# Layer 0's cross attention: scores from queries taken through the key weights, against the context itself

## The reference

```python
xn = _layernorm(x, ln_gamma, ln_beta)
q = (xn @ w_q).reshape(B, SQ, NUM_HEADS, DIM_HEAD)
kv = context @ w_kv
k, v = jnp.split(kv, 2, axis=-1)
scores = jnp.einsum('bqhd,bkhd->bhqk', q * SCALE, k)
attn = jax.nn.softmax(scores, axis=-1)
out = jnp.einsum('bhqk,bhkd->bqhd', attn, v).reshape(B, SQ, INNER)
out = out @ w_out + b_out
return out * jnp.tanh(gate[0])
```

## Time and profile before

| | us |
|---|---|
| median of 3 runs | 1728.44 (1726.32 to 1729.37) |
| the profiled execution | 1730.11 |
| its span, first to last instruction | 1728.2 |
| start of the first matmul | 9.08 |
| first scores of the attention loop | 65.55 |
| scores of the 31st unit | 488.65 |

### The profile page before, as it was taken

The page is one execution under the profiler, slowest core; times in us unless marked ns, Lnnn a source line. Parts: engine busy times, 40 slices in busy tenths (PEclk is TensorE's granted clock), DMA queues, the critical chain, the costliest instruction groups (busy, mean ns, idle before and its releaser), DMA issues.

```text
span 1728.2 us, 27121 instructions
## 1 busy us (share of the span) xinstructions
PE 1679.0 (97%) x10603; PEld 1290.0 (75%) x10603; DVE 980.5 (57%) x1999; ACT 791.9 (46%) x1564; POOL 234.0 (14%) x317
## 2 busy tenths in 40 slices
PE   7999999999999999998999999999999899999997
PEld 5577777777757766564999986677767678799996
DVE  4243344434346686522766665565554776598885
ACT  3333333333324345520655564454445443477774
POOL 0100000000001301313111102211100304021111
PEclk9999999999999999999999999999999999999999
DMA  6020110102042003033999973111231052599994
GB/s 252 1 98 30 45 45 30 49 26 75 24 159 98 1 1 120 28 124 134 343 389 389 392 273 104 32 62 34 84 123 49 25 213 101 206 354 363 362 363 105
DMA packets 43805, 246.52 MB, mean 143 GB/s; under 512 B 5801, under 2 KB 6305, under 8 KB 20624
## 3 DMA queue, kind: packets, MB, share of 16 engines
q1 hardware_dynamic: 31392, 216.63, 33.3%
q0 software_dynamic: 7664, 19.68, 4.1%
q10 hardware_dynamic: 4608, 8.33, 1.3%
HBM read 229.01 MB, written 16.13 MB: 142 GB/s over the span
## 4 chain that ended last, share of the span: by engine, by line
PE 92%; DVE 3%; DMA 2%; ACT 1%; issue 1%; POOL 1%; SPq 0%; POOLq 0%; DVEq 0%; ACTq 0%
PE bank L648 29%; PE bank L268 12%; PE bank L2380 7%; PE bank L274 5%; PE bank L791 3%; PE bank L3453 3%; PE bank L819 3%; PE bank L745 2%; PE bank L2931 2%; PE bank L1490 2%; PE bank L738 2%; PE bank L1174 2%; PE bank L1989 2%; PE bank L1991 2%; PE bank L1990 2%; PE bank L1547 1%
## 5 line engine op out<-in xcount | busy, mean ns | idle before, releaser
L648 PE MATMUL bank<-split 128*128 128x512 f32 x2196 | 530.4, 396 | 1.3 <-ACT arena L674 1.3
L648 PEld LDWEIGHTS bank<-split 128*128 128x128 f32 x2196 | 404.3, 188 | 99.3 <-issue 9.5
L268 PE MATMUL bank<-arena,weights 128*128 128x128 f32 (+1 forms) x1032 | 136.1, 290 | 10.8 <-DMA weights<-in_L_xattn_w_kv 9.1
L268 PEld LDWEIGHTS bank<-arena,weights 128*128 128x128 f32 x1032 | 123.8, 193 | 24.3 <-issue 12.9
L799 ACT COPY normed<-bank 128x512 f32<-128x512 f32 x128 | 68.9, 592 | 150.4 <-PE bank L791 150.4
L762 DVE TENSOR_REDUCE small<-bank 128x1 f32<-128x512 f32 x64 | 43.9, 686 | 151.8 <-PE bank L738 151.8
L680 DVE COPY arena<-bank 128x512 f32<-128x512 f32 x76 | 52.5, 691 | 120.8 <-PE bank L648 120.8
L674 ACT COPY arena<-bank 128x512 f32<-128x512 f32 x76 | 44.5, 586 | 152.8 <-PE bank L648 114.3
L2380 PE MATMUL bank<-up_high_r,tok_r 128*128 128x352 f32 x512 | 108.2, 323 | 0.0
L274 PE MATMUL bank<-weights,arena 128*128 128x512 f32 x224 | 101.7, 604 | 0.9 <-issue 0.9
L781 ACT ACTIVATE normed<-bank,small 128x512 f32<-128x512 f32 x64 | 44.1, 689 | 124.0 <-DVE small L764 123.7
(11 more groups left out here) (404 smaller groups left out, 3092.6 us busy)
## 6 DMA issues: line engine op xcount, KB each, us to landing
weights<-in_L_ffn_re_w SPq DMA_DIRECT2D x62, 1024.0 KB, 10.6
weights<-in_L_w SPq DMA_DIRECT2D x20, 1408.0 KB, 13.1
arena<-in_ctxT SPq DMA_DIRECT2D x24, 1024.0 KB, 5.0
arena<-in_L_w SPq DMA_DIRECT2D x12, 1408.0 KB
weights<-in_L_w_full SPq DMA_DIRECT2D x10, 1280.0 KB, 10.6
weights<-in_L_ffn_sw SPq DMA_DIRECT2D x9, 1024.0 KB, 4.7
expert_out<-arena ACTq DMA_DIRECT2D x31, 256.0 KB, 8.3
arena<-in_L_w_full SPq DMA_DIRECT2D x6, 1280.0 KB
```

The lines of the kernel that those rows point to most:

```text
L268: s = pe.matmul(out, w[:, k, j0:j0 + m], rhs(k), start=(k == 0), stop=(k == KT - 1))
L648: s = pe.matmul(bank[:, :], still, moving, start=(n == 0), stop=(n == len(order) - 1))
```

## The change

Instead of projecting the context to keys, the kernel multiplies the queries by the transposed key weights of each head. What comes out, `through_keys` (for each sequence and head 512 x 64, split into halves), is the stationary side of the scores, and the split context itself is the moving side. The scores are thus the same sums in another order.

- The host lays the key half of `w_kv` out transposed and by rows (`L0_xattn_w_kT`), the value half as before (`L0_xattn_w_v`).
- Key groups g = 0 to 3 are gone in layer 0; each unit projects two value groups.
- `through_keys_tensor(c, z)` is new: 16 fp32 matmuls with 64 rows x 128 columns of key weights stationary and a head's 64 queries moving. Even heads are on rows 0 to 63, odd heads on rows 64 to 127, into two banks. Two such calls make a step's operand; ACT and DVE split each bank into high and low halves (entries "qw" of the split order). In the loop each call is made for the step after the present one.
- `scores_tensor` makes two groups of 12 matmuls 128 x 512, one for each of banks 3 and 4, each with its own count in `scored`. A head pair now lies in one bank, where before each bank held every second head.
- On DVE the values copy and the "qw" low halves stand ahead of the value groups' copies; the context of the next step but one is split in one go in each step's second unit.
- The start: context 0 and the first value weights come in eight slices of 256 KB with a semaphore each; value groups of step 0 are computed slice by slice into banks 0 to 3 (`first_values_tensor`). x, query and key weights are asked for right behind. All four value groups stand ahead of the transposes, and queries with two through_keys calls between them behind.
- The second half of the key weights is loaded behind context 9, once the calls of steps 0 to 7 are done.

```diff
+            for k in range(2):
+                for m in range(KT):
+                    for s in range(2):
+                        r, o = s * half, (k * KT + m) * SEQ
+                        last = pe.matmul(halves[s][:, o:o + SEQ], w.view[r:r + half, m, (2 * z + k) * P:(2 * z + k + 1) * P],
+                                         self.qT[r:r + half, self.tile_of(c, m), b * SEQ:(b + 1) * SEQ], start=True, stop=True)
+            last.then_inc(self.qw_mm.sem, 1)
...
+                order = [(k, a, b) for k in range(KT) for a, b in ((0, 0), (0, 1), (1, 0))]
+                for i in range(2):
+                    m = 2 * u + i
+                    if n >= 1:
+                        pe.wait_ge(self.exped.sem, self.exped.at(2 * n - 1 + i))
+                    for j, (k, a, b) in enumerate(order):
+                        last = pe.matmul(banks[3 + i][:, :], self.through_keys[c % 2][a][:, k, m * P:(m + 1) * P],
+                                         self.split_ctx[c % 2][b][:, k, :], start=(j == 0), stop=(j == len(order) - 1))
+                    last.then_inc(self.scored.sem, 1)
...
-                        last = pe.matmul(banks[3 + s][i * half:(i + 1) * half, :],
-                                         self.qT[r:r + half, self.tile_of(c, 2 * u + i), b * SEQ:(b + 1) * SEQ],
-                                         self.kT[c % len(self.kT)][r:r + half, 2 * u + i, :], start=True, stop=True)
...
+                if self.layer == 0 and c + 1 < self.steps:
+                    self.through_keys_tensor(pe, c + 1, u)
...
+                    if c == NSEQ + 1:
+                        sp.wait_ge(self.qw_mm.sem, self.qw_mm.at(2 * NSEQ))
+                        load_weight(sp, "x0_k1")
...
-        x0.load_context(sp, 0)
-        load_weight(sp, "x0_k0")
-        load_weight(sp, "x0_v0")
-        sp.wait_ge(x0.kv_mm.sem, x0.kv_mm.at(1))
-        sp.wait_ge(x0.low.sem, x0.low.at(x0.ctx_split(0)))
-        x0.load_context(sp, 1)
+        values = weights["x0_v0"]
+        for k in range(KT):
+            c = slice(k * DIM, (k + 1) * DIM)
+            sp.dma_start(x0.ctxT[:, k, :], A["ctxT"][0][:, k, :]).then_inc(slice_in[k], 16)
+            sp.dma_start(wslot[values.slot][:, c], values.source[:, c]).then_inc(slice_in[KT + k], 16)
         for i in range(NT):
             sp.dma_start(x[:, i, :], A["x"][:, i, :]).then_inc(x_in[i], 16)
         load_weight(sp, "x0_q0")
+        load_weight(sp, "x0_k0")
         load_weight(sp, "x0_q1")
+        sp.wait_ge(x0.low.sem, x0.low.at(x0.ctx_split(0)))
+        x0.load_context(sp, 1)
...
+        x0.first_values_tensor(pe)
         pe.wait_ge(consts, IDENT)
...
-        for g in (2 * KT - 2, 2 * KT - 1):
-            x0.kv_tensor(pe, 0, g)
         pe.wait_ge(first_xnT, KT)
-        x0.queries_tensor(pe, range(x0.tiles))
+        x0.queries_tensor(pe, range(5))
+        x0.through_keys_tensor(pe, 0, 0)
+        x0.queries_tensor(pe, (5,))
+        x0.through_keys_tensor(pe, 0, 1)
+        x0.queries_tensor(pe, (6, 7))
```

More of the change, by code:

```diff
@@ L540, in __init__ @@
                 if layer == 0:
-                    count = KT
-                    splits = [("ctx", c + 2, 2 * u), ("ctx", c + 2, 2 * u + 1)]
+                    count = KT // 2
+                    splits = [("qw", c + 1, u, s) for s in range(2)] + [("ctx", c + 2, k) for k in range(KT) if u == 1]
                 else:
@@ L651, in kv_bank, with first_values_tensor, through_keys_tensor @@
         def kv_bank(self, c, g):
+            if self.layer == 0 and c == 0:
+                return banks[g - KT]
             return banks[self.place["kv", c, g] % 3]
+        def first_values_tensor(self, pe):
+            for k in range(KT):
+                pe.wait_ge(self.low.sem, self.low.at(self.split_no["w", "v", 0, k]))
+                for g in range(KT, 2 * KT):
+                    for a, b in ((0, 0), (0, 1), (1, 0)):
+                        s = pe.matmul(self.kv_bank(0, g)[:, :], self.split_ctx[0][a][:, k, (g - KT) * P:(g - KT + 1) * P],
+                                      self.split_v[b][:, k, :], start=(k == 0 and a == b == 0), stop=(k == KT - 1 and a == 1))
+                    if k == KT - 1:
+                        s.then_inc(self.kv_mm.sem, 1)
+        def through_keys_tensor(self, pe, c, z):
+            w = weights[f"x0_k{c // NSEQ}"]
+            if c % NSEQ == 0:
+                pe.wait_ge(w.landed, w.value)
+                pe.wait_ge(self.q_a.sem, self.q_a.at(self.tile_of(c, KT)))
+            halves = [self.bank_free(pe, self.place["qw", c, z, s]) for s in range(2)]
+            b, half = c % NSEQ, P // 2
+            for k in range(2):
[5 more added lines that the diff above has]
+            last.then_inc(self.qw_mm.sem, 1)
         def kv_out(self, e, c, g, bank):
-            e.wait_ge(self.kv_mm.sem, self.kv_mm.at(2 * KT * c + g + 1))
+            e.wait_ge(self.kv_mm.sem, self.kv_mm.at(self.per_step * (c + 1) - 2 * KT + g + 1))
             if g < KT:
```

177 lines of the change are left out of this document (110 added, 67 removed), and 2 rows, old and new, of the table LOADS.

## The result

| | before | after |
|---|---|---|
| median, us | 1727.38 (1725.39 to 1729.37, 4 runs) | 1755.16 (1754.49 to 1757.98, 4 runs) |
| span of the profiled execution | 1728.2 | 1752.3 |
| first matmul | 9.08 | 7.08 |
| first scores of the attention loop | 65.55 | 58.43 |
| a unit of the loop | 14.14 | 15.03 |

The changed kernel takes 1.0164 times as long, interval 1.015 to 1.0179: 27.8 us more. The forecast was 1758 in 1743 to 1774, slower. Direction, size and nearly every term held. The runs were needed for why the calls cost what they do, how much of the start is in the two parts of the change, and why the profiled spans differ by only 24.1.

A forecast was written before the change was run, and what follows sets the result against it. The prediction took TensorE, busy 97% of the span, to bound the kernel. Its terms, 9.2 + 27.6 - 7.75 + 0.8 = +29.9, added to 1728.4, gave 1758 us, range 1743 to 1774 for 8 in 10.

The forecast's parts named there:

- What bounds: Whole kernel: TensorE is busy 97% of the span, so a change counts by what it adds to or takes from TensorE's queue.
- Part 1: Attention loop: new scores replace key projection at equal cost in units 0 to 29; the last two units add 9.2 us.
- Part 2: Units 0 to 29: each through_keys call, bound by loads, takes 1.94 us against old scores' 1.02; +27.6 us in all.
- Part 3: Ahead of the loop: sliced loads start TensorE at 7.0, first scores at 57.8 instead of 65.55; -7.75 us.
- the clock: At the start, after about 3 us idle before the queries: lower granted clock costs 0 or about 1.7; 0.8 us taken.
- Part 4: Unit 13: the second half of the key weights lands late for its call; +0.8 us, bounds 0 and 4.
- What stays hidden: Each unit: added ACT casts and DVE subtractions stay under TensorE's work; without this cover a unit would pay up to 1.4.
- B: The 32 calls: moving columns, not loads, set the pace; 1.08 us a call, 27.5 less, total 1731; 8%.
- C: The calls: a tile can't take new weights while its own matmul runs; 2.8 us a call, total 1786; 5%.
- D: Every unit: TensorE waits 0.5 us for a bank or low half from DVE; 16 us, total 1774; 9%.
- The sum: Whole kernel: 9.2 + 27.6 - 7.75 + 0.8 = +29.9 us, added to the median 1728.4 for 1758 us.

The follow-up runs named there:

- the two runs on the call: Changed kernel with 64 of 128 stationary columns in each through_keys matmul: 1734.3 us; changed kernel with 128 moving columns instead of 64: 1757.27 us.
- covered: Changed kernel with the fourth first value group moved behind the transposes, where TensorE stood idle before the queries: 1755.11 us, ratio 1.0141 to the kernel before.
- covered again: The changed kernel with its fourth value group behind the transposes, run once more beside the changed kernel: 1755.12 us, ratio 1.0159 to the kernel before.
- changed again: The changed kernel run once more, unaltered, for a second trace: 1756.25 us, ratio 1.0176 to the kernel before.
- 34 and 17 dummies: Kernel before with 34, or 17, added fp32 matmuls between the last two query tiles, outputs unchanged: 1762.21 us (ratio 1.0202) and 1742.85 us (1.008).
- slices: Kernel before with context 0 and first value weights loaded in eight slices, value groups first, keys still projected: 1729.02 us, ratio 0.9984.
- before again: The kernel before run once more, unaltered, for a second trace: 1728.03 us.
- slices fitted: Kernel before with sliced first loads, x requested ahead of key weights, key splits behind the statistics, all key groups behind the transposes: 1725.8 us, ratio 0.9984.

## Why the prediction was right, point by point

- **What bounds** (the sum is a difference in PE's queue): right. At the mark the sum of PE's rows and the measured shift agree, in part by luck: the 30 units cost 0.5 more than the rows of one unit give, and what follows them 0.4 less.
- **Part 1** (+9.2): 9.1.
- **Part 2** (1.94 a call, +27.6): 1.93 and +26.7 in the 30 units. The new unit was put at 15.06 and is 15.03. The reason given, loads on two row tiles side by side, each tile at the pace of its own, is what the two runs on the call confirm. The clearest evidence ahead of time was the pair of rows where the columns of the load changed and the time with them.
- **Part 3** (-7.75): 7.1. First matmul 7.08 for 7.0, transposes 20.26 for 20.6, queries 25.31 for 25.6, so the idle time of 3.14 for about 3 was right. The term that was mis-sized is the clock: I took 0.8 between 0 and 1.7, and both traces of the changed kernel have the full fall. The row to go by was the earlier trace rows, the nearest in length of the idle time, and halving its price was hedging in the sum what belongs in the range. The prediction gives no row for the 1.7; the trace of before bears it out, with 6.9 us lost in four falls behind the mark. These 0.9 more, less the 0.3 by which the queries began earlier than 25.6, are the 0.6 by which the first scores came later than 57.8. And the 65.55 from which the term is taken is the latest start of four traces, so the other pair gives 5.7.
- **Part 4** (+0.8): 0.3, within its bounds of 0 and 4.
- **What stays hidden**: right. PE waits in no unit but the one where the key weights come 0.3 late. On DVE the low halves of the call and the four context splits are done and the next maxima still wait 2.6 us for the scores, as two rows of DVE's timeline in such a unit show (L746 the last value copy, L832 the maxima):

```profile
117.55 0.68 DVE L746 COPY arena<-bank 128x512 f32<-128x512 f32 x1
120.86 0.69 DVE L832 TENSOR_REDUCE small<-bank 128x1 f32<-128x512 f32 x1 [2.63 <-PE bank L803]
```

- **The rivals**: B is what happens when the loads are made half as wide (1.08 a call), so its price was right and its condition was not met: it spoke of half the rows, and the load follows the columns. C would show at 128 moving columns and doesn't. D does not occur.
- **The sum**: +29.9 predicted, +29.0 and +30.7 at the mark in the two pairs of traces, +27.8 in the medians of the first comparison and 30 by the ratio of the second. The last step, that nothing behind the stage changes, is right on the medians. It is not right on a single span, where waits and clock of the later part move it by up to 8.5 us. I had given that no term and, on two spans, no warning.

## What to carry to other kernels

Exchanging one product for another by associativity is decided by how the new product sits on the array: 16 matmuls with 64 rows, 128 columns and only 64 moving columns cost 1.93 us, 1.8 times what the same count costs with 64 columns stationary (1.08), because the fp32 loads set the pace. All else in a unit was an exchange of equals, 24 matmuls for 24, so a call had to be cheaper than the old scores' 1.02 us. Even with calls of 1.08 the mark was at 561.9, later than the 559.7 of the kernel before. Cost such small matmuls by their loads, per row tile and by columns. And compare kernels at a mark just behind the change as well as at the end: here the mark gave the change to within 2 us, while a single span could be off by several. What the clock and the waits take can be subtracted.

## What the runs showed of the hardware

- Two row tiles side by side load fp32 weights each at 0.107 us for 128 columns (an estimate, from a call's 1.93 less 0.23, over 16), and 64 or 128 moving columns hide under it: 1.93 and 1.98 us for 32 halves. With 64 stationary columns the same takes 1.08.
- After 1.9 us of transposes and 3.14 us without work the granted clock fell to 0.50 in both traces of the changed kernel, for a loss of 1.7 us. With the idle time at 0.41 or 0.38 (covered, covered again) it stayed at 1.00.
- In one and the same row, a product with 8 columns moving behind an idle time of 0.19 us, the clock falls for a shorter stretch, for one twice as long, or not at all: the row takes 4.57 in changed, changed again, with 128 columns moving and with 64 stationary; 6.26 in before, covered and with 34 and 17 dummies, 6.25 with the slices; 7.92 in before again and covered again, 7.94 with the slices fitted. What decides it I don't know.
- The wait of 4.26 us at the expert lists is in three of the twelve traces (4.3 before, 4.0 covered, 4.6 slices); four others wait 0.35 to 1.59 at the same place and five not at all. The nine without the long wait wait 1.4 to 2.4 for a DMA of token rows a little later, the three with it don't. Of two executions of the same kernel one has the long wait and one has not.
